# Graph network in four layers: edge attributes carried by the first sort and summed in the first edge stage

## The reference, cut to what matters

```python
# first layer, twice
msg = x[src] * ew[:, None]
agg = jax.ops.segment_sum(msg, dst, num_segments=n)
...
# third layer
aggregated = jax.ops.segment_sum(edge_attr, dst, num_segments=num_nodes)
node_input = jnp.concatenate([node_feat, aggregated], axis=-1)
h = node_input @ W1 + b1
```

## Time and profile before

| | us |
|---|---|
| median of 3 runs (4824.14 to 4830.65) | 4827.94 |
| profiled execution | 4823.27 |
| its span | 4821.5 |
| front: from the start to the first `hit` of l0a | 419.2 |
| stage l0a: 419.2 to 704.7 | 285.5 |
| stage l2: 2354.35 to 2636.6 | 282.2 |

### The profile page before, as it was taken

The page is one execution under the profiler, slowest core; times in us unless marked ns, Lnnn a source line. Parts: engine busy times, 40 slices in busy tenths (PEclk is TensorE's granted clock), DMA queues, the critical chain, the costliest instruction groups (busy, mean ns, idle before and its releaser), DMA issues.

```text
span 4821.5 us, 94015 instructions
## 1 busy us (share of the span) xinstructions
PE 3775.1 (78%) x18956; PEld 2297.9 (48%) x18956; DVE 3546.8 (74%) x13545; ACT 2185.7 (45%) x4510; POOL 3181.8 (66%) x3644
## 2 busy tenths in 40 slices
PE   4652789968899868899778889998578775787776
PEld 1221338833455523566433778888333442234443
DVE  8874646676487864576743788888887888887888
ACT  0000353314588844455335344444236564265666
POOL 4655757767599977333575566666576777775787
PEclk6876999989999989999899999999799998899999
DMA  1001468834688744688546455555356885477676
GB/s 24 10 8 36 131 207 275 279 104 149 213 272 259 233 133 153 222 270 272 168 129 209 131 166 172 165 169 164 107 164 219 251 249 172 144 222 238 222 236 198
DMA packets 481460, 861.31 MB, mean 179 GB/s; under 512 B 86745, under 2 KB 91584, under 8 KB 481048
## 3 DMA queue, kind: packets, MB, share of 16 engines
q1 hardware_dynamic: 335370, 596.71, 39.2%
q10 hardware_dynamic: 85310, 155.79, 8.8%
q0 software_dynamic: 60368, 104.48, 8.4%
HBM read 532.31 MB, written 324.36 MB: 178 GB/s over the span
## 4 chain that ended last, share of the span: by engine, by line
PE 30%; DVE 20%; issue 13%; POOL 12%; DVEq 7%; DMA 5%; SPq 3%; ACT 1%; POOLq 1%; ACTq 0%
PE ps L1425 10%; POOL got L635 7%; DVEq L65 6%; DVE hit L975 4%; DVE stat L1022 4%; PE ps L1548 3%; PE ps L1547 3%; PE ps L1453 2%; PE ps L1557 2%; DVE hid L1123 2%; POOL x2T L651 2%; POOL rstd L671 2%; DVE mv L1028 2%; PE ps L1485 2%; PE ps L1484 2%
## 5 line engine op out<-in xcount | busy, mean ns | idle before, releaser
L671 POOL TENSOR_TENSOR rstd<-vare,neg_half 128x4 f32<-128x4 f32 x686 | 698.8, 1019 | 627.5 <-DVE vare L1035 624.6
L1425 PE MATMUL ps<-hit,got 128*128 128x512 bf16 x1758 | 701.1, 399 | 476.0 <-DVE hit L975 310.9
L1199 ACT ACTIVATE evac<-ps 128x512 f32<-128x512 f32 x588 | 351.2, 597 | 1001.9 <-PE ps L1425 984.5
L1425 PE MATMUL ps<-hit,rest 128*128 128x512 bf16 x1758 | 702.6, 400 | 0.0
L1425 PE MATMUL ps<-hit,tail 128*128 128x512 bf16 x1758 | 700.8, 399 | 0.0
L1223 ACT ACTIVATE xout<-res,shift,rstd 128x128 f32<-128x128 f32 x1176 | 482.8, 485 | 431.5 <-POOL shift L674 411.9
L1425 PEld LDWEIGHTS ps<-hit,got 128*128 x1758 | 178.0, 101 | 855.2 <-issue 712.2
L1063 DVE TENSOR_TENSOR nT<-sums,ps 128x512 f32<-128x512 f32 x490 | 336.1, 686 | 325.0 <-PE ps L1463 269.6
L635 POOL DMA_INDIRECT got<-nodes_l,sorted_by_dst x392 | 395.5, 1009 | 164.5 <-issue 108.2
L975 DVE TENSOR_SCALAR hit<-node_of,node_at_dst 128x512 bf16<-128x512 f16 x1465 | 438.2, 367 | 19.3 <-POOLq L394 10.0
L1004 DVE TENSOR_TENSOR rest<-got 128x512 f32<-128x512 f32 x294 | 204.7, 696 | 240.2 <-DMA got<-in_edge_attr,sorted_by_dst 112.6
(11 more groups left out here) (264 smaller groups left out, 9163.2 us busy)
## 6 DMA issues: line engine op xcount, KB each, us to landing
nodes_l<-xout SPq DMA_DIRECT2D x196, 256.0 KB, 3.0
xin<-nodes_l SPq DMA_DIRECT2D x196, 256.0 KB, 2.7
sums_l<-evac ACTq DMA_DIRECT2D x196, 256.0 KB
sums<-sums_l SPq DMA_DIRECT2D x196, 256.0 KB
sums_l0a<-evac ACTq DMA_DIRECT2D x98, 256.0 KB
sums<-sums_l0a SPq DMA_DIRECT2D x98, 256.0 KB
sums_l0b<-evac ACTq DMA_DIRECT2D x98, 256.0 KB
sums<-sums_l0b SPq DMA_DIRECT2D x98, 256.0 KB
```

The source lines that it names most:

```text
L671: pool.tensor_tensor(rstd[:, n, at, :], vare[:, n, at, :], neg_half[:, :], ALU.pow)\
L1199: act.activation(evac[:, slot, :], ps[:, g % BANKS, :], ACT.Copy).then_inc(s["out"].sem, 1)
L1425: last = pe.matmul(into, part.rearrange("p a d -> p (a d)"), hit[:, i % HITS, :], start=False, stop=False, skip_group_check=True)
```

## The change

The records of the sort by `dst` grow from 8 to 8 + 128 words: each carries its edge's attribute row, 544 bytes in all. In the front ScalarE's queue loads the attributes by batches (`attr_parts`) into a ring of eight, `row`; GpSimd copies the 8 words beside them (in the place of memset and drain) and scatters from there. The sorted table is read back as before, but the 8 words now lie 544 bytes apart. In l0a a second ring of tiles is loaded by SyncE's queue from the sorted table, four tiles per DMA, in order, and VectorE, TensorE and ScalarE do for it what they do for the first: six matmuls per step in place of three, into two banks. Its sums go to the table that d2b reads. Stage l2 is gone. To make room, the two `member` tiles of the front become one, and `HITS` is 96 and the evacuation ring 3 in l0a (`Window`). The stages after l0a are the same but for their numbers.

```diff
-RECORD = {"dst": FIELDS, "src": FIELDS}
+RECORD = {"dst": FIELDS + D, "src": FIELDS}
...
+        def attr_parts(b):
+
+            v, full, k = t["edge_attr_128"], FULL_PARTS * TILES, b * K
+            held = row[:, b % ROW_RING, :, FIELDS:FIELDS + D].bitcast(F32)
+            parts = [(held[0:FULL_PARTS, :, :], v[0:full, :].rearrange("(p k) d -> p k d", k=TILES)[:, k:k + K, :])]
+            if k + K <= REST:
+                parts.append((held[FULL_PARTS:FULL_PARTS + 1, :, :], v[full + k:full + k + K, :].rearrange("(a k) d -> a k d", a=1)))
+            return parts
+
+        def rows_in(b):
+
+            return 16 * sum(1 + (i * K + K <= REST) for i in range(b % ROW_RING, b + 1, ROW_RING))
...
+                if BUFFERS[name].pair:
+                    attr = rec_d["dst"].rearrange("(p k) f -> p k f", p=P)
+                    for b in range(BATCHES):
+                        if b >= 4:
+                            sp.wait_ge(*s["free"](b - 3))
+                        at = b * K % RING
+                        sp.dma_start(paired.got[1][:, at:at + K, :].bitcast(I32), attr[:, b * K:b * K + K, FIELDS:FIELDS + D])\
+                          .then_inc(s[f"pair{b % 4}"].sem, 16)
...
-                pool.memset(pause[:, :], 0.0)
-                pool.drain()
+                pool.wait_ge(s_row[b % ROW_RING], rows_in(b))
+                pool.tensor_copy(row[:, b % ROW_RING, :, 0:FIELDS], record[:, b * K:b * K + K, :]).then_inc(s_joined, 1)
+                held(s_joined, b + 1)
+                return lambda k: row[:, b % ROW_RING, k % K, :]
...
                         held(s["step"].sem, free[j % 4] & 511)
+                        if BUFFERS[name].pair:
+                            pool.sem_inc(s["free"].sem, 1)
...
-                    dve.tensor_tensor(four(rest, b), four(got, b), upper(got_hi, b), ALU.subtract)
+                    if w.pair:
+                        dve.wait_ge(*s[f"pair{b % 4}"](16 * (b // 4 + 1)))
+                    for n in range(1 + w.pair):
+                        dve.tensor_tensor(four(w.rest[n], b), four(w.got[n], b), upper(w.got_hi[n], b), ALU.subtract)
                     dve.drain()
-                    dve.tensor_tensor(four(tail, b)[:, :, 0:D], four(rest, b), upper(rest_hi, b), ALU.subtract).then_inc(s["msg"].sem, 1)
+                    for n in range(1 + w.pair):
+                        last = dve.tensor_tensor(four(w.tail[n], b)[:, :, 0:D], four(w.rest[n], b), upper(w.rest_hi[n], b), ALU.subtract)
+                    last.then_inc(s["msg"].sem, 1)
...
+            for b in range(BATCHES):
+                if b >= ROW_RING:
+                    act.wait_ge(s_scat[b % 4], 64 * (b // 4 - 1))
+                for part, ap in attr_parts(b):
+                    act.dma_start(part, ap).then_inc(s_row[b % ROW_RING], 16)
...
+                halves = ((0, sum_d[name]), (1, sum_d["l2"]))[0:1 + w.pair]
+
+                def clear(g):
+
+                    for h, _ in halves:
+                        last = act.activation(ps[:, BANKS * h + g % BANKS, :], zeros[:, :], ACT.Copy)
+                    last.then_inc(s["zero"].sem, 1)
...
-                    act.activation(evac[:, slot, :], ps[:, g % BANKS, :], ACT.Copy).then_inc(s["out"].sem, 1)
-                    act.wait_ge(*s["out"](g + 1))
+                    for h, _ in halves:
+                        act.activation(w.evac[h][:, slot, :], ps[:, BANKS * h + g % BANKS, :], ACT.Copy).then_inc(s["out"].sem, 1)
+                    act.wait_ge(*s["out"](len(halves) * (g + 1)))
                     if g + BANKS < GROUPS:
-                        act.activation(ps[:, g % BANKS, :], zeros[:, :], ACT.Copy).then_inc(s["zero"].sem, 1)
-                    act.dma_start(sum_d[name][g * P:(g + 1) * P, :], evac[:, slot, :]).then_inc(s[f"st{slot}"].sem, 16)
-                for slot in range(EVAC):
-                    act.wait_ge(*s[f"st{slot}"](16 * len(range(slot, GROUPS, EVAC))))
+                        clear(g)
+                    for h, dest in halves:
+                        act.dma_start(dest[g * P:(g + 1) * P, :], w.evac[h][:, slot, :]).then_inc(s[f"st{slot}"].sem, 16)
...
-                    into = ps[:, bass.ds(bank, 1), :].rearrange("p a n -> p (a n)")
-                    for part in (got_hi[:, bass.ds(slot, 1), 1:2 * D:2], rest_hi[:, bass.ds(slot, 1), 1:2 * D:2],
-                                 tail[:, bass.ds(slot, 1), 0:D]):
-                        last = pe.matmul(into, part.rearrange("p a d -> p (a d)"), hit[:, i % HITS, :], start=False, stop=False,
-                                         skip_group_check=True)
+                    for h in range(1 + w.pair):
+                        into = ps[:, BANKS * h:BANKS * h + BANKS, :][:, bass.ds(bank, 1), :].rearrange("p a n -> p (a n)")
+                        for part in (w.got_hi[h][:, bass.ds(slot, 1), 1:2 * D:2], w.rest_hi[h][:, bass.ds(slot, 1), 1:2 * D:2],
+                                     w.tail[h][:, bass.ds(slot, 1), 0:D]):
+                            last = pe.matmul(into, part.rearrange("p a d -> p (a d)"), w.hit[:, i % w.hits, :], start=False, stop=False,
+                                             skip_group_check=True)
                     last.then_inc(s["step"].sem, 1)
...
-            edges("l2", 7)
-            nodes(8, d2b)
+            nodes(7, d2b)
```

## The result

| | before | after |
|---|---|---|
| median of the runs, us | 4826.04 (4822.43 to 4830.65) | 4971.15 (4968.69 to 4972.44) |
| profiled execution, us | 4823.3 | 4971.85 |
| its span, us | 4821.5 | 4970.0 |
| front ends (first `hit`), us | 419.2 | 712.2 |
| l0a, us | 285.5 | 412.8 |

The ratio is 1.030, with a 95% interval of 1.0282 to 1.0317: +145 us where +324 was forecast. The direction, the range and the mechanism of the front held; the size did not.

A forecast was written before the change was run, and what follows sets the result against it. Stages are bounded separately, the front by its scatter, then by attribute loads on one DMA engine: 4823.3 + 437.8 (front) + 166.1 (l0a) - 282.3 (l2) = 5144.9 us, 5150 at the median; range 4890 to 5430.

The forecast's parts named there:

- The direction: Whole kernel: slower by more than 0.2%, chance 0.91.
- the range: Whole kernel: a time of 4890 to 5430 us.
- the mechanism of the front: Front: attribute loads of 127 partitions get one DMA engine, 16.1 us per batch; front +437.8 us.
- the size: Whole kernel: +324 us, to 5150 us.

The follow-up runs named there:

- e7: Kernel before with TensorE's wait numbers loaded for four fours of steps at once instead of two, on a slower chip: 5116.0 us, ratio 0.9992.
- f2: Changed kernel with each attribute load of 127 partitions split into 112 and 15, on a slower chip: 4893.93 us, ratio 0.9573 to the kernel before.

## What to carry to other kernels

Look at a load's partition count before its bytes: 127 partitions went through one DMA engine at 25 ns per 512-byte piece, and splitting them into 112 and 15 was worth 325 us (295 on a slower chip). Price a stream of small packets by the time from one to the next in a row where the stream is dense, not by a packet's busy time, and keep a gap only if the work that might hide it stays the same. And a rest on GpSimd's queue may be what keeps VectorE running on some chips: an edit that takes one away has to be timed on more than one chip.

## What the runs showed that I had not expected

- Two kinds of chips: the same kernel at 4823 to 4825 us on two and 5118 to 5123 on the others. There (e7) the front is 4 us longer, each of the six edge stages 38 to 45, and the first node stage, in which GpSimd scatters by `src`, 50; the other node stages are the same.
- On the slower ones, scatters issued every 1.26 us leave VectorE one small operation per 1.4 us (busy 11.4 of 100 us, against 96.2); a rest of about 0.8 us per five operations of GpSimd (f2) gives back most, 67.6 of 100, and one of 2 us all of it (e7, 95.7).
- The busy times of 25,104 packets of a queue sum to 139% of 16 engines.
- A granted clock of 0.89 in place of 0.92 in a stage whose instructions are the same, and which is 13 us longer.
